# Second attention of a two-layer tower: two of eight row tiles masked in place, the output copied by another engine, and loads asked for in another order

## The reference

```python
draft = einsum('bhqd,bhkd->bhqk', qr, kr) + causal          # 2 x 32 heads, 1024 x 1024
num_remain = max(min(Sq, 128), Sq - int(Sq * 0.9))           # 128
_, keep = top_k(draft, num_remain)
mask = neg everywhere, 0 at keep
attn = softmax(draft_scaled + mask); out = attn @ v; out @ Wo.T
...
scores = 8 * softmax(x @ Wr.T + br)                          # second mixture
out = einsum('bsd,hrd', x, A) weighted by scores, @ Bm
```

## Time and profile before

| | |
|---|---|
| time, median of 3 (lowest to highest) | 4969.97 us (4964.9 to 4971.59) |
| profiled execution, its time | 4971.85 us |
| its span | 4969.9 us |
| mean granted TensorE clock | 0.865 |
| busy: TensorE, VectorE, ScalarE, GpSimd | 4028.0, 3258.2, 2802.1, 570.6 us |

### The profile page before, as it was taken

The page is one execution under the profiler, slowest core; times in us unless marked ns, Lnnn a source line. Parts: engine busy times, 40 slices in busy tenths (PEclk is TensorE's granted clock), DMA queues, the critical chain, the costliest instruction groups (busy, mean ns, idle before and its releaser), DMA issues. The chain is left out here.

```text
span 4969.9 us, 85458 instructions
## 1 busy us (share of the span) xinstructions
PE 4028.0 (81%) x25611; PEld 2331.5 (47%) x25752; DVE 3258.2 (66%) x9570; ACT 2802.1 (56%) x6546; POOL 570.6 (11%) x1877
## 2 busy tenths in 40 slices
PE   6998999999999989954777467766777777776899
PEld 2445766667444444422444234433444444443454
DVE  3555777777233345548877887887787888786244
ACT  1114777777000001147888588888888888887100
POOL 1000000000000000002122121221221221222000
PEclk8999999999999999976787677777877777777899
DMA  3326322222211113221111011111011111010542
GB/s 143 78 67 168 81 56 72 66 68 64 94 51 51 54 34 78 67 56 22 28 28 25 4 28 28 25 28 28 5 28 28 28 25 28 10 22 6 135 111 78
DMA packets 308441, 260.38 MB, mean 52 GB/s; under 512 B 188672, under 2 KB 242704, under 8 KB 307920
## 3 DMA queue, kind: packets, MB, share of 16 engines
q1 hardware_dynamic: 307376, 254.32, 20.1%
q0 software_dynamic: 544, 0.07, 0.0%
HBM read 176.21 MB, written 78.12 MB: 51 GB/s over the span
## 5 line engine op out<-in xcount | busy, mean ns | idle before, releaser
L1086 ACT ACTIVATE a_sign<-arena,a_state 128x384 fp8e4<-128x384 f32 (+5 forms) x1056 | 917.6, 870 | 88.6 <-DVE a_state L1259 50.2
L980 PE MATMUL a_ps_s<-k,q 128*128 128x512 bf16 (+3 forms) x1475 | 390.4, 397 | 401.5 <-DVE arena L1361 260.0
L992 PE MATMUL a_ps_t<-ident,arena 128*128 128x128 f32 x1584 | 343.6, 335 | 258.4 <-ACT a_probT L1054 244.4
L1054 ACT ACTIVATE a_probT<-a_ps_t 128x512 f32<-128x512 f32 (+3 forms) x768 | 363.9, 478 | 244.4 <-PE a_ps_t L999 238.9
L1086 ACT ACTIVATE a_sign<-a_third,a_state 128x384 fp8e4<-128x384 f32 (+2 forms) x480 | 417.2, 871 | 71.9 <-DVE a_state L1298 59.2
L738 ACT ACTIVATE a_prob<-a_x_neg,a_shift 128x640 f32<-128x640 f32 (+7 forms) x512 | 397.2, 776 | 90.0 <-DVE a_x_neg L781 63.4
L980 PEld LDWEIGHTS a_ps_s<-k,q 128*128 128x128 bf16 x1536 | 145.7, 115 | 560.9 <-DVE arena L1361 289.6
L781 DVE TENSOR_SCALAR_CACHE_REDUCE a_x_neg<-a_ps_s 128x640 f32<-128x640 f32 (+7 forms) x512 | 378.6, 751 | 41.9 <-PE a_ps_s L662 26.2
L677 PE MATMUL a_ps_t<-ident,a_prob 128*128 128x128 f32 x2304 | 365.0, 282 | 35.9 <-issue 16.3
L1309 DVE MAX8 a_nine<-a_below 128x8 f32<-128x256 f32 (+6 forms) x448 | 371.0, 828 | 34.4 <-issue 1.7
L1018 PE MATMUL a_ps_o<-a_probT,vals 128*64 128x128 f32 x4608 | 393.0, 316 | 0.0
(11 more groups left out here) (262 smaller groups left out, 7169.3 us busy)
## 6 DMA issues: line engine op xcount, KB each, us to landing
q<-qk SPq DMA_DIRECT2D x256, 256.0 KB, 4.6
qk<-p_qkT SPq DMA_DIRECT2D x32, 960.0 KB, 6.2
h_rows<-h SPq DMA_DIRECT2D x32, 512.0 KB, 6.8
k<-qk SPq DMA_DIRECT2D x256, 64.0 KB, 4.9
h<-tok_h SPq DMA_DIRECT2D x16, 512.0 KB, 4.0
arena<-in_wo SPq DMA_DIRECT2D x16, 512.0 KB, 6.4
o<-a_o SPq DMA_DIRECT2D x16, 512.0 KB, 2.7
q<-o SPq DMA_DIRECT2D x16, 512.0 KB, 5.5
```

The source lines that it names most:

```text
L980: nc.tensor.matmul(score(n)[:, a:a + w], q[:, y, head, i * P:(i + 1) * P], k[:, y, a:a + w], start=(y == 0), stop=False, skip_group_check= ...
L992: nc.tensor.matmul(to[:, c:c + P], xs[old][:, at:at + P], ident[:, :], start=(c == 0), stop=False, is_transpose=True, skip_group_check=True)
L1054: nc.scalar.activation(probT[:, n % 4, 0:w], ps_t[:, (n + 1) % 2, 0:w], ACT.Exp).then_inc(probT_ready, 1)
L1086: ins = nc.scalar.activation(to, xs[mine][:, at:at + w], ACT.Sign, scale=-1.0, saturate=False, bias=state[:, par, 0, n:n + 1], accum_out=s ...
```

## The change

Six edits, the first four in the second attention:

1. Row tiles 6 and 7 have no bf16 mask any more. `mark` rewrites their scores in place on VectorE, as `(x < limit) - x` in f32, and ScalarE's Exp gets a scale of the other sign for them. All scores are stored times 2^-13, so that the 1 stands for a large number after the scale. TensorE leaves out the mask matmuls of those tiles (30 of 70 in a slot).
2. Marks: tile 6 goes with tiles 1 to 5 in pass 2, tile 7 stays in pass 3, and `exact_where_needed` moves from pass 2 to pass 3, behind the marks of tile 7. VectorE's wait for the chunks of tile 6 is gone. One increment of `masked` replaces the fourteen of `mask_ready`.
3. The copy of the output goes from VectorE, end of pass 3, to ScalarE, end of pass 4. TensorE waits for it before the first values, not before the first chunk.
4. The values of the next group are asked for as soon as the last values of this group are done, ahead of the last stores of the group; before, they were asked for after those stores had landed.
5. GpSimd no longer negates the maxima; the sign is in the row that TensorE multiplies with, which costs twelve small instructions on VectorE once, at the start of the stage.
6. In the last mixture the weights `ar`, `bT` and `bias` are asked for right after the first `h`, the first `o` and its inverse sums.

```diff
@@ turn (TensorE)
+                        by_mask = i and not TURNS_OVER(i)
                         mm = nc.tensor.matmul(to.rearrange("p (b c) -> p b c", c=P), row_of[:, m * TT + i, :],
                                               topT[:, :].unsqueeze(1).to_broadcast([SPLITS * 2 * TT, w // P, P]),
-                                              start=False, stop=(i == 0), skip_group_check=True)
-                        for c in range(0, w if i else 0, P):
+                                              start=False, stop=not by_mask, skip_group_check=True)
+                        for c in range(0, w if by_mask else 0, P):
@@ slot (TensorE)
-                        pe.wait_ge(mask_ready, (s - 2) * NS + NS)
-                        if not (isinstance(s, int) and s == 2):
-                            pe.wait_ge(o_ready, s - 2)
+                        pe.wait_ge(masked, s - 1)
...
+                            if n == 2 and not (isinstance(s, int) and s == 2):
+                                pe.wait_ge(o_ready, s - 2)
@@ ScalarE
+                    def output():
+                        act.wait_ge(pv_done, (s - 2) * (NC // 2) + NC // 2)
+                        if not (isinstance(s, int) and s == 2):
+                            act.wait_ge(o_out, (s - 2) * 64)
+                        nc.scalar.copy(o[:, :], ps_o[:, :]).then_inc(o_ready, 1)
...
+                        if p == PASSES - 1 and st["value"]:
+                            output()
@@ mark (VectorE)
+                        if TURNS_OVER(i):
+                            nc.vector.scalar_tensor_tensor(out=old_x[:, at:at + w], in0=old_x[:, at:at + w],
+                                                           scalar=limit[:, r:r + 1], in1=old_x[:, at:at + w], op0=ALU.is_lt,
+                                                           op1=ALU.subtract)
+                        else:
+                            nc.vector.tensor_scalar(mask[:, at:at + w], old_x[:, at:at + w], limit[:, r:r + 1], MASKED,
+                                                    ALU.is_lt, ALU.mult)
@@ part (VectorE), pass 2 then pass 3
-                                if st["value"]:
-                                    dve.wait_ge(turn_done, (s - 2) * TURNED + wide_turned)
-                                for r in KEEPS[1][0:2]:
-                                    mark(r).then_inc(mask_ready, 1)
-                                exact_where_needed()
...
+                                for r in KEEPS[1]:
+                                    mark(r)
+                                exact_where_needed()
+                                dve.sem_inc(masked, 1)
...
-                        if p == 3 and st["value"]:
-                            output()
@@ group (SyncE)
+                        if more and y == PPG - 1:
+                            wait_alone(sp, pv_done, (g * PPG + PPG) * (NC // 2), const_in, 48)
+                            load_values(sp, g + 1, v[:, :, 0:DH], v_dram, v_in)
@@ last_mixture (SyncE)
-                for j in range(RING):
-                    if j:
-                        load_o(j)
-                    load_h(j)
-                compact_rows(sp, 1, compact, total_dram, inverted, True)
-                sp.dma_start(bias[:, :], bias_dram.partition_broadcast(P)).then_inc(rest_in, 16)
+                load_h(0)
+                load_o(1)
                 sp.dma_start(ar[:, :, :], ar_dram.rearrange("(k p) n -> p k n", p=P)).then_inc(rest_in, 16)
                 sp.dma_start(bT[:, :], b_dram).then_inc(rest_in, 16)
+                sp.dma_start(bias[:, :], bias_dram.partition_broadcast(P)).then_inc(rest_in, 16)
+                load_h(1)
+                compact_rows(sp, 1, compact, total_dram, inverted, True)
+                for j in range(2, RING):
+                    load_o(j)
+                    load_h(j)
```

More of the change, by code:

```diff
@@ L1195, in _ @@
                 nc.vector.memset(code[:, :], 0.0)
-                nc.vector.memset(floor[:, :], MASKED)
+                nc.vector.memset(floor[:, 0:1], MASKED)
+                nc.vector.memset(floor[:, 1:2], -MASKED)
                 nc.vector.memset(marked[:, :], 0.0)
@@ L1204, in _ @@
                 nc.vector.tensor_tensor(rows[:, :], rows[:, :], of[2], ALU.add)
+                dve.drain()
+                for m, i in TILES:
+                    if not TURNS_OVER(i):
+                        only = rows[:, m * TT + i:m * TT + i + 1]
+                        nc.vector.tensor_scalar(only, only, -1.0, None, ALU.mult)
                 dve.drain()
@@ L1343, in select_exactly @@
                         nc.vector.tensor_scalar(lost, left, TAKEN / 2, None, ALU.is_gt)
-                        nc.vector.memset(limit[:, n:n + 1], ALL_KEPT)
+                        if not over_:
+                            nc.vector.memset(limit[:, n:n + 1], ALL_KEPT)
                         dve.drain()
-                        nc.vector.copy_predicated(old_x[:, at:at + w], lost, floor[:, :].to_broadcast([P, w]))
+                        nc.vector.copy_predicated(old_x[:, at:at + w], lost,
+                                                  floor[:, over_:over_ + 1].to_broadcast([P, w]))
                         dve.drain()
@@ L1360, in fetch @@
                         dve.wait_ge(s_done, (s + 1) * (2 * TT) + (n + 1))
-                        nc.vector.tensor_scalar(new_x[:, at:at + w], score(n)[:, 0:w], 1.0, None, ALU.mult, ALU.max,
+                        nc.vector.tensor_scalar(new_x[:, at:at + w], score(n)[:, 0:w], DOWN, None, ALU.mult, ALU.max,
                                                 accum_out=top[:, m * TT + i:m * TT + i + 1]).then_inc(x_ready, 1)
-                    def output():
-                        dve.wait_ge(pv_done, (s - 2) * (NC // 2) + NC // 2)
-                        if not (isinstance(s, int) and s == 2):
-                            dve.wait_ge(o_out, (s - 2) * 64)
-                        nc.vector.tensor_copy(o[:, :], ps_o[:, :]).then_inc(o_ready, 1)
                     def scale_first():
@@ L1396, in slot @@
                     by_row = [RANKED.index(r) for r in RISING if r[1]]
-                    KEEPS = [n for n in range(NS) if RANKED[n][1] < HALF], [n for n in by_row if RANKED[n][1] >= HALF]
+                    KEEPS = [n for n in range(NS) if RANKED[n][1] < TT - 1], [n for n in range(NS) if RANKED[n][1] == TT - 1]
                     AT_ONCE, MORE, LATE = range(0, 4), range(4, 6), range(12, 2 * TT)
@@ L1437, in part @@
                             if st["keep"]:
-                                for r in KEEPS[1][2:]:
-                                    mark(r).then_inc(mask_ready, 1)
+                                for r in KEEPS[1]:
+                                    mark(r)
+                                exact_where_needed()
+                                dve.sem_inc(masked, 1)
                             if st["score"]:
```

30 lines of the change are left out of this document (12 added, 18 removed).

## The result

| | before | changed |
|---|---|---|
| time, median of 11 each (lowest to highest) | 4967.94 us (4957.73 to 4971.59) | 4984.42 us (4980.67 to 5074.3) |
| ratio of the two, 95% interval | | 1.0039, 1.0030 to 1.0048 |
| profiled span | 4969.9 us | 4981.1 us |
| mean granted TensorE clock | 0.865 | 0.861 |

The changed kernel is 0.39% slower by the ratio (16.5 us between the medians), and lies 17 us over the upper end of the predicted range. (One execution of the changed kernel, at 5074.3 us, ran at a clock of 0.823 and is left out of the ratio.)

A forecast was written before the change was run, and what follows sets the result against it. In the second attention TensorE, often at 1.2 GHz, brings chunks late to ScalarE, notably in pass 2. Terms -8.6 - 3.5 + 3 + 1.5 + 1 - 1.4 - 2.0 - 10.9 = -20.9 us gave 4950 us, range 4930 to 4967.

The forecast's parts named there:

- The step that failed: Second attention, slot 8: the long exact selection moves from pass 2 to pass 3 and loses overlap, +1.5 us (0 to +3).
- Mask matmuls, -8.6 and -3.5: Pass 2: without mask groups ScalarE waits less, 0.33 us at chunk 16 in 26 slots, 0.16 at chunk 23 in 22.
- the sign that was named: Pass 2, slot 12: chunk 16's wait about 0.3 us under 2.32, where the clock dips as before.
- The output on ScalarE, +3: End of pass 4: a copy of 1.03 us, less 0.91 us of waiting for VectorE, +0.1 us a slot over 30.
- The marks, +0.94 a slot in pass 3: VectorE, tile 7: two marks in the new form take 2.35 us instead of 1.41.
- The branch: VectorE, pass 3: 2.7 us of sequencer, 2.35 covered by the marks; net +0.1 to +0.4 against 1.41 idle, so nothing.
- rival 3: VectorE late in pass 3 because the branch isn't covered, +1.0 us a slot, 30 us: 4981; chance 7%.
- Early values, nothing: Second attention's loop: asking earlier for the next group's values gains nothing, since no TensorE wait there names them.
- Slots 32 and 33, -1.4 and -2.0: After the loop: slot 32's first transpose starts sooner without waiting for the output's copy; slot 33 loses eight mask groups.
- Last mixture, -10.9: Weights land before the second projection ends; transposes and `down` follow without a gap, third projection at 4683.4 instead of 4694.31.
- rival 2: The clock falls once more in a slot, in pass 2 after chunk 16, 2.0 us a slot: +39, 5010; chance 8%.
- Rival 4: The clock gains: pass 2's dip vanishes in a third of 26 slots, or the loop's phase moves: 4932; chance 12%.

The follow-up runs named there:

- a_magic: The changed kernel with the first guess of the inverse root in the search's start shifted by 4096 units in the last place; 4929.76 us, ratio 0.9923.
- a_same: The changed kernel with the search's start computed as in the kernel before, one more small VectorE instruction a slot; 4934.24 us, ratio 0.9942.
- a_nosel: The changed kernel with the exact selection's branch never taken, failing rows left as they are; 4875.77 us, ratio 0.9827.
- b_scaled: The kernel before with only scores stored times 2^-13, Exp's scale 2^13 and the variance's small constant 1e-28; 5012.85 us, ratio 1.0101.
- a_nudge: The changed kernel with the last limit of every row multiplied by 1 + 2^-23, one unit in the last place; 4946.04 us, ratio 0.9953.
- a_best: a_same with the search's first limits set 0.1% further from the mean; 5021.8 us, ratio 1.0105.
- a_mm: a_same with TensorE's 30 mask matmuls of row tiles 6 and 7 put back, with masks of zeros; 4939.97 us, ratio 0.995.
- a_out_dve: a_same with the copy of the output back on VectorE at the end of pass 3; 4970.94 us, ratio 1.001.
- b_vearly: The kernel before with only the next group's values asked for ahead of the last stores; 4965.6 us against 4968.23, ratio 0.9994.
- b_nosel: The kernel before with the exact selection's branch never taken, failing rows left as they are; 4916.14 us, ratio 0.9906.
- b_tail: The kernel before with only the last mixture's loads in the new order; 4953.24 us against 4963.89, ratio 0.998.

## Why the prediction was wrong

It forecast 4950 us, 4930 to 4967, with a chance of 0.10 for slower. The time was 4984.4.

**The step that failed** is the one that said of slot 8: "In slot 8 the long exact selection runs in pass 2; moved, it no longer overlaps what it overlapped: +1.5 us (0 to +3)." Its size came out as 3.1 us in slot 8 of the profile; by the medians the one selection costs 48.3 us before and 54.0 to 58.5 after (`a_magic` and `a_same`, which has one more instruction in each slot, over `a_nosel`), so it may be a few us more. What the step left out is that the number of such selections is not fixed. The scaling was put at nothing, without a word on it; it is exact for the scores but not for the search's start, and a limit that falls on a score costs some 50 us. `b_scaled` shows the cause, `a_same` its price in the changed kernel (50.2 us), `a_nudge` its kind. That the new start met one score in this input, and not none or three as in `a_best`, is chance. Neither the sum nor a rival had it, so the range didn't either. Without it the time is 4934.2 us, inside the range and 16 us under the forecast, or 4929.8, at the range's lower end, by `a_magic`.

**Mask matmuls, -8.6 and -3.5.** The wait at chunk 23 fell by 0.17 us a slot in all thirty (0.16 in 22 was forecast; that chunk had waited 0.75 us or more in all thirty before). At chunk 16 the sign that was named didn't show: in slot 12 the wait rose from 2.32 to 2.51 us. Over the thirty slots its mean fell from 1.87 to 1.48. In pass 2 the gain was larger than forecast, 23.0 us without selections. But as the worth of the missing matmuls -12.1 was too much: putting them back costs 5.7 us at the medians (`a_mm`), and in the profiles what their absence saves at chunk 16 is lost at chunks 6 and 7. The rows at one place were right, the step from a place to the stage wasn't.

**The output on ScalarE, +3.** The price was right: 0.99 us in the timeline, with no idle time left around it. The sign of the edit was wrong, because it was held against VectorE's idle time of before. With marks of 2.48 us instead of 1.41 and the branch in pass 3, VectorE has no 1.2 us for a copy; leaving it there costs 36.7 us (`a_out_dve`).

**The marks, +0.94 a slot in pass 3:** measured 2.48 - 1.41 = 1.07. **The branch:** 0.65 us show before the first fetch, between the 0.35 worked out and the 2.7 of the rival. The idle time of 0.8 to 1.3 us that was said to be left is 0.2 to 0.9 in most slots, and none in eight; in slot 12 VectorE is 0.4 us late. So rival 3, VectorE late in pass 3, is there, at some 1.2 us over all slots instead of 30; the gaps in which VectorE waits for TensorE's scores between its fetches (0.31 and 0.35 us in slot 12) were in neither sum. It comes true in full in `a_out_dve`.

**Early values, nothing:** right for the kernel before (`b_vearly`), and the price of its absence, 82 us with the copy in its new place, was not asked for. No wait in the profile before could show it; that the stores now end after pass 4 could have.

**Twelve small instructions:** 0.9 us between the stage's first instruction and the first fetch; +1 was forecast.

**Slots 32 and 33, -1.4 and -2.0:** the transpose at 4605.08 is the first of slot 33, not of slot 32, which the prediction took it for: the last work of slot 32, the transpose of `a_top_parts`, stands just before it. It starts 0.6 us earlier against the last limits of slot 31 and not 1.4, since it now waits for the flag's code. From there to the mixture's first projection it is 39.1 us and was 45.2. The stretch before, and then after:

```profile
4605.08:4650.25 45.17, 40.57 (x311) 25.47 (x311) 4.11 (x3) 11.77 (x24) 0.00 (x0) 0.77 0.44 135
```

```profile
4632.85:4671.96 39.11, 34.76 (x280) 21.65 (x281) 2.98 (x2) 12.78 (x25) 0.00 (x0) 0.85 0.50 145
```

The -6.1 is mostly luck with the clock, 0.77 in the one profile and 0.85 in the other. `b_nosel`, with the same code here as before, took 40.80 us at 0.875; the six profiles with the attention of before took 43.0 us in the mean, the seven with the change's whole attention 39.7. That makes -3.2, over the -2.0 of the forecast.

**Last mixture, -10.9:** -10.86 in the profile (17.93 against 28.79), -10.65 by `b_tail`. The transposes took 1.04 and `down` 2.12 us, full clock, as worked out. The second inverse sums landed 14.6 us behind the first, within the 13.1 to 17.3 worked out, and the third projection didn't wait for them.

**The rivals.** The clock's second dip, rival 2, did not come in pass 2, where it was priced: without selections that pass was granted 0.901 before and 0.899 after. It came in pass 3, where TensorE isn't waited for, and cost nothing; `a_mm`, with the mask matmuls back, has it too (0.87 in slot 13), so it isn't for want of them. The Trainium skill, "TensorE: Matmul & The Clock Gate", section "Part 4: PE-mode transpose", by which transposes don't bring full clock, would have made pass 2 slower with a larger share of transposes in it. Here it doesn't come out so: pass 2 got 23.0 us shorter in sum at nearly the same mean clock. Rival 4, a dip that vanishes in some slots, is partly there: ScalarE's wait at chunk 16 is absent in 5 of 30 slots of `a_nosel` and over 1.3 us in 19 (before it was absent in 4, slots 3, 9, 23 and 30). One reading of the trace before was off beside this: its slots last from 70.2 us (slot 9), not from 71.5.

Not settled: where the rest of the gain in the attention comes from. `a_same` is 19 us under `b_tail`, and without selections the attention gives some 30 (40.4 less 10.65). Of this 5.7 belong to the mask matmuls and some 3 to slot 33, in part the same. The remainder, 10 to 20 us, goes with VectorE's lost wait and copy and the other edits, which weren't tried alone.

## What to carry to other kernels

Where a kernel has a slow path that data opens, the number of times it is taken is a term of the sum: count it in the trace before, look for every edit that changes a rounding on the way to its condition, and leave room for one more and one less. Here one is worth 1% of the time, more than all the edits together, so measure such a kernel with the path shut as well (`b_nosel` against `a_nosel`) before an edit is judged.

Price an edit against the kernel as it will be with the others in it: the early load is worth 82 us beside the other edits and nothing in the kernel before, and the late copy, which had been priced as a loss of 3 us, is worth 37 beside them.

A wait at one chunk that a few matmuls end is not worth its length times its count in such a loop: what one pass gives, the next may take back. And a small idle time in front of an instruction is spare only if it ends on another engine; where it ends on "issue", the engine is the late one.

## What the runs showed of the hardware

A mark of 128 x 1024 in f32, read twice and written in place by `SCALAR_TENSOR_TENSOR`, took 1.24 us (2.48 for two in a row), as much as a product in place of the same width (1.23); a bf16 result from one such stream took 0.71. Multiplying all scores by 2^-13 is exact, yet the search's start, an inverse root that begins with arithmetic on the bits of a float, came out otherwise: that alone made 48 us here (`b_scaled`), and working it out at the old exponent took them away (`a_same`). Putting 30 matmuls a slot back, 0.23 us and more for each of eight groups, cost 5.7 us over thirty slots, not eight times thirty times 0.23 = 55; that most of them fill time in which TensorE would wait for ScalarE fits this, but wasn't shown. In pass 3 TensorE's longest idle stretch grew from 1.35 to 3.33 us (slot 13), and the clock of the pass fell from 1.00 to 0.87, with no loss of time, since other engines set its length.
